# GpSimd's FFN sums wait for the square-sum of the next move's middle state

## What is computed

```
def rms(z): return z / sqrt(mean(z*z) + EPS)
O_lh, O_rh = polar_orthogonal(W_lh), polar_orthogonal(W_rh)      # 12 iterations each
q = xn @ Wq.T ; v = xn @ Wv.T
def step(h, q_t):
    h_new = rms(h @ O_lh.T + q_t @ O_rh.T)
    return h_new, h_new
Y = (qs * v) @ Wc.T
real = xn @ cos(theta + theta_noise)
imag = xn @ sin(phi + phi_noise)
out = x + Y + sqrt(real*real + imag*imag)
```

## Time and profile before

| | |
|---|---|
| median of 3 runs | 140.2 us (140.16 to 141.63) |
| profiled execution, its own time | 140.24 us |
| its span, first to last instruction | 138.4 us |
| busy in the span | PE 116.6 us (84%), DVE 103.2 (75%), ACT 76.4 (55%), POOL 55.1 (40%) |
| granted TensorE clock, mean | 0.998 of full |

### The profile page before, as it was taken

One profiled execution on the slowest core, in us unless ns is written; L12 is line 12 of the kernel. 1 busy time (PEld: TensorE's weight loads), 2 busy tenths in 40 slices (PEclk: granted clock), 3 DMA queues, 4 the chain that ended last, 5 costly groups with the idle time before them and its releaser, 6 DMA issues.

```text
span 138.4 us, 2697 instructions
## 1 busy us (share of the span) xinstructions
PE 116.6 (84%) x775; PEld 91.5 (66%) x775; DVE 103.2 (75%) x411; ACT 76.4 (55%) x284; POOL 55.1 (40%) x92
## 2 busy tenths in 40 slices
PE   6988898789999999999999967788878888788861
PEld 6766777689966666666666644577756767577740
DVE  3579999984476777777777777578887877878862
ACT  4035999997546666666556566643534334353430
POOL 7302786850024444445555544553232322323220
PEclk9999999999999999999999999999999999999999
DMA  4884000000000000000000000001020220202211
GB/s 123 236 247 174 0 0 7 0 0 0 5 0 2 0 0 0 0 5 0 0 0 0 5 0 0 2 5 69 7 76 0 81 76 2 76 0 81 76 38 40
DMA packets 3342, 4.95 MB, mean 36 GB/s; under 512 B 448, under 2 KB 1344, under 8 KB 3328
## 3 DMA queue, kind: packets, MB, share of 16 engines
q1 hardware_dynamic: 3024, 4.46, 9.9%
q0 software_dynamic: 160, 0.26, 0.7%
q10 hardware_dynamic: 144, 0.07, 0.2%
HBM read 2.69 MB, written 2.10 MB: 35 GB/s over the span
## 4 chain that ended last, share of the span: by engine, by line
PE 45%; DVE 39%; ACT 6%; issue 6%; DVEq 1%; POOL 0%
DVE W L679 8%; PE bank L947 7%; DVE SQM L665 7%; PE bank L906 7%; PE bank L938 5%; DVE VT L702 5%; PE bank L954 4%; DVE WMID L660 4%; PE bank L862 4%; DVE WTM L686 3%; DVE bank L673 3%; PE bank L846 3%; PE bank L957 2%; PE bank L790 2%; PE bank L785 2%
## 5 line engine op out<-in xcount | busy, mean ns | idle before, releaser
L293 POOL TENSOR_TENSOR FS<-FSQ 128x256 f32<-128x256 f32 x16 | 11.6, 724 | 36.9 <-ACT FSQ L423 36.9
L906 PE MATMUL bank<-IDENT,W 128*128 128x128 f32 x31 | 10.1, 327 | 11.2 <-DVE W L679 11.1
L408 ACT ACTIVATE SQE<-W 128x129 f32<-128x129 f32 x32 | 10.0, 313 | 15.6 <-DVE W L679 15.6
L286 POOL TENSOR_SCALAR XN<-X,MV,RSTD 128x128 f32<-128x128 f32 x16 | 13.5, 847 | 11.8 <-DVE RSTD L563 11.8
L906 PEld LDWEIGHTS bank<-IDENT,W 128*128 128x128 f32 x31 | 4.3, 139 | 19.6 <-DVE W L679 19.6
L929 PE MATMUL bank<-CS,XNT 128*128 128x256 f32 x64 | 16.5, 380 | 0.0
L790 PE MATMUL bank<-ONES 128*128 128x128 bf16 x158 | 16.1, 219 | 0.0
L640 DVE COPY WT<-bank 128x128 f32<-128x128 f32 x30 | 8.7, 292 | 9.2 <-PE bank L906 9.2
L947 PE MATMUL bank<-WCT,PV 128*128 128x128 f32 x64 | 14.6, 310 | 0.7 <-POOL PV L317 0.6
L954 PE MATMUL bank<-PXT,WT 128*128 128x128 f32 x60 | 14.6, 325 | 0.0
L317 POOL TENSOR_TENSOR PV<-VT,WTM 128x128 f32<-128x128 f32 x16 | 7.3, 453 | 18.3 <-DVE WTM L686 18.3
(11 more groups left out here) (170 smaller groups left out, 286.7 us busy)
## 6 DMA issues: line engine op xcount, KB each, us to landing
X<-in_L_attn_x_dram SPq DMA_DIRECT2D x8, 256.0 KB, 6.9
out_dram<-OUT SPq DMA_DIRECT2D x7, 256.0 KB, 2.0
out_dram<-OUT SPq DMA_DIRECT2D x2, 128.0 KB, 1.7
WP<-in_L_attn_W_rh_dram ACTq DMA_DIRECT2D x1, 64.0 KB, 1.9
WP<-in_L_attn_W_lh_dram SPq DMA_DIRECT2D x1, 64.0 KB, 2.2
ANG<-in_L_ffn_theta_dram POOLq DMA_DIRECT2D x1, 64.0 KB, 3.5
WV<-in_L_attn_Wv_dram SPq DMA_DIRECT2D x1, 64.0 KB, 3.3
ANG<-in_L_ffn_phi_dram POOLq DMA_DIRECT2D x1, 64.0 KB, 3.2
```

The lines of the kernel that those rows point to most:

```text
L286: pool.tensor_scalar(XN[:, t, :], X[:, t, :], MV[:, t, 0:1], RSTD[:, t:t + 1], ALU.subtract, ALU.mult).then_inc(S["xn_pool"], 1)
L293: pool.tensor_tensor(FS[:, f % 2, :, :], FSQ[:, f % 2, :, 0:P], FSQ[:, f % 2, :, P:2 * P], ALU.add).then_inc(S["ffn_sum"], 1)
L906: pe.transpose(TB[:, 0:P], W[:, 0:P], IDENT[:, :]).then_inc(t_done, 1)
```

## The change

POOL, ahead of the FFN sum of item f, waits until `ssm_ready` has counted f + 2, that is until the sum of squares of WMID of move f + 1 is there. It does so for the items 0 to 14. Item 15 has no such wait. Nothing else is changed: the same instructions run on the same data in the same order on each engine.

```
             for f in range(STEPS // 2):
+                if f + 1 < GUESSES:
+                    pool.wait_ge(ssm_ready, f + 2)
                 ffn_sum(f)
                 if f:
                     ffn_added(f - 1)
```

## The result

The changed kernel takes 135.19 us, the median of 4 runs (134.51 to 135.34), against 140.69 us for the kernel before on the same chip (4 runs, 140.16 to 141.63). The ratio is 0.9593, with a 95% interval of 0.9524 to 0.9661: 4.1% faster. The forecast was 134.6 us in a range of 134.0 to 136.3.

What follows compares the result with a forecast made beforehand. The prediction took a chain of waits through DVE's square-sum, held by POOL's FFN sum, as the bound. Gains of 13 x 0.41 = 5.3 and 0.24 us took 140.24 to 134.6 us, range 134.0 to 136.3.

Steps and rivals of the forecast that it cites:

- SQM is held by POOL's FS: On DVE, the square-sum over which POOL's FFN sum runs ends 0.15 to 0.16 us after that sum, taking 0.71, not 0.30.
- The rival that SQM's length is not POOL's doing: On DVE, something other than POOL lengthens the square-sum, so the time stays 140.2 us; chance 0.05.
- The size of a hold, 0.42 a move: Square-sum to W falls from 1.06 to 0.64 us in moves 2 to 14; 5.46 us if all reaches the next move.
- The wait of item 14: In move 15 the square-sum already takes 0.29 us, so this wait gains nothing.
- the 14 that were named as a sign: Expected in the profile after: 14 of 16 FS starting 0.1 us or so after the square-sum is read.
- PE takes over: Before the transpose, PE becomes the limit once DVE is earlier, allowing a gain of 0.41 us a move.
- The rival at 137.1 us: PE limits the moves at its modelled end, giving 0.24 us a move, not 0.41; chance 0.09.
- POOL's queue: After the wait POOL runs FS, then XF, and is silent 0.94 us before the next square-sum.
- The hold does not move to line 673: On DVE, line 673 and W stay at 0.35 us under FS, at no cost.
- The slower rival: FS holds line 673 instead, delaying W 0.19 us a move, 2.7 us in all, 142.9 us; chance 0.04.
- The rule that was weighed: Full blocking of the square-sum by FS would lengthen holds about 0.14 us a move, giving about 132.9 us; not followed.
- The sum: 5.3 us from 13 moves plus 0.24 for move 1, 5.6 off 140.24, gives 134.6 us.

Runs made afterwards that it cites:

- E1: The changed kernel run again with no edit: 134.8 us, 0.9571 of the kernel before.
- E3: The changed kernel with POOL's wait one instruction earlier, on the middle state itself (`mid_ready`): 135.34 us, 0.961 of the kernel before.
- E2: The changed kernel with the wait kept only on the odd items 1 to 13: 137.58 us, 0.9761 of the kernel before.
- E5: The kernel before, without the wait, with POOL fills that read nothing in place of the FFN sums: 135.9 us, 0.9698 of the kernel before.
- E9: The kernel before, without the wait, with each FFN sum cut into two halves: 136.79 us, 0.9744 of the kernel before.
- E8: The kernel before with added waits ahead of the FFN sums of items 0 to 14, on an event long past: 141.34 us, 1.0072 of the kernel before.
- E4: The changed kernel with POOL's wait moved later, to the next move's transposed state in SBUF (WT): 138.91 us, 0.9858 of the kernel before.
- E7: The changed kernel with 0.22 us more PE work in each FFN item: 137.0 us, 0.9759 of the kernel before.
- E6: The kernel before with 0.22 us more PE work in each FFN item: 140.59 us, 1.0011 of the kernel before.

## Why the prediction was right, step by step

*SQM is held by POOL's FS.* Shown from several sides: it vanishes where FS comes later (after, E1, E3), in exactly the moves where it does (E2); it is not there with fills in place of the sums (E5, with the limits named there); it shrinks with FS's length (E9), grows when FS starts later and still first (E8), and comes back under XF (E4). Wherever SQM was held it ends 0.14 to 0.17 us after the POOL instruction that began first, in all these traces. The rival that SQM's length is not POOL's doing is refuted by this.

*The size of a hold, 0.42 a move.* Measured 5.70 us over the moves 1 to 15, against 0.25 + 13 x 0.42 = 5.71 as the full sum. The wait of item 14 gave nothing, as forecast, but it does hold FS back as the others do: 15 of the 16 sums start 0.09 us after the square-sum is read, not the 14 that were named as a sign.

*PE takes over.* The step that chose 0.41 of a possible 0.42 by the starts of matmuls, not 0.24 by their modelled ends, holds: the period is 2.77 us, where the modelled ends as a bound give 3.19 - 0.24 = 2.95, and E7 puts PE's own period at some 2.73. The rival at 137.1 us is refuted. Idle time of PE read from modelled ends was short by 0.16 us; the spacing of starts in a move where PE was the late one gave the real room. It was close all the same: the room that was left is some 0.04 us a move.

*POOL's queue.* FS 0.09 after the sum (forecast 0.08), silence before the next SQM 0.97 (0.94), XF of no harm. E4 is what happens when this cover is gone: XF holds SQM in FS's place, as the prediction said, and it cost 0.29 a move.

*The hold does not move to line 673.* The slower rival is refuted, though the trace of the changed kernel alone would not do it for this line, since the line starts 0.17 us ahead of FS there. In E3 it starts 0.17 us behind FS's start and takes 0.35, and W takes 0.35 under FS in both.

*The rule that was weighed.* The Trainium skill, "SBUF — State Buffer", section "SBUF: two separate sides", has the later one wait for the whole of the earlier. The prediction took this to mean that the whole length of the held one follows, and the traces differ from that in the size on both sides: a held SQM ends 0.15 us after FS, half of its own 0.30, and a held FS in E3 is longer by 0.11 where 0.24 of SQM were left. What the same page says in "Who interferes with whom" agrees with the runs: a GpSimd instruction that only writes does not collide with two SBUF inputs (E5, a fill beginning behind SQM keeps its 0.31), and a `tensor_scalar` from SBUF to SBUF may (DIAG in E4, 0.70 for 0.29).

*The sum.* 134.6 was forecast and 135.19 measured, and the gain, against 140.69 for the kernel before beside it, is 5.50 where 5.6 was forecast. That the two gains agree so well is in part luck: the moves gave 5.70 in the profiled run, 0.1 more than the sum (0.42 a move and not 0.41), and 0.62 + 0.22 us were lost at the start and the end, where the sum had nothing.

Are these losses the change's? The tail's is not: it is absent in E1, and E6, which has no added wait, shows it too (4.53 us). For the start-up, the starts of SQM of move 0 and the times point different ways. The starts are 37.21 to 37.46 in the six traces with a sum held back (37.46 and 37.23 for the changed kernel itself), and 36.85, 36.87, 36.97, 37.02 and 37.19 in the five without (36.87 is E8, which has waits). Each is one execution, and by them alone the late start would seem to go with the moved sum. The times speak against a cost. Over all executions on record the kernel before has a median of 140.57 us and a least of 140.16 (38 executions), the changed one 134.91 and 134.51 (10 executions). The differences, 5.66 and 5.65, are the 5.70 of the moves, so little or nothing is lost outside of them on the whole. Why the early products on PE are slow for a different time in each execution stays open, as does why the late starts fall on these six traces.

## What to carry to other kernels

Where one shape of a DVE instruction has two durations, look at what POOL reads over it: here the end of the long ones followed the end of a POOL instruction by a constant 0.15 us. It cost nothing to let the engine that has time start second, by 0.05 us (E3) or by 0.38 (the changed kernel), as long as it had fallen silent before the next such instruction (E4); cutting its work into shorter instructions gave part of the gain without a wait (E9). Read PE's room from the spacing of starts, and settle a tie on the chain by adding a little work to one side.

## What the runs showed that was not expected

- A satisfied wait added in front of a POOL instruction's own waits delayed it by 0.05 to 0.07 us, and it made the kernel 0.7% slower (E8), since POOL's sum was the one that DVE waited for.
- A DVE instruction with one tensor from SBUF, written to SBUF, is held too: 0.70 us for 0.29 (E4). Those with one tensor from SBUF and one from PSUM never were, 0.34 to 0.36 us in every trace.
- The first 8 us of the span differ by up to 0.6 us between traces of the same instructions there (0.23 between the two of the changed kernel), by products on PE that run slower for longer under a granted clock that reads 1.00.
